# Attention and a mixture of experts on one core: the second LayerNorm's root and scaling on GpSimd, earlier projections, and the first scores among the last expert tiles

## The chip, the cores and the metric

The kernel runs on 1 core of one Trainium2 chip. The metric is the device time of one execution in microseconds; of the kernel before there are three runs, with a median of 300.53 us (299.96 to 301.22). Engines are named as the profile names them: PE (TensorE matmuls), PEld (its weight loads), DVE (VectorE), ACT (ScalarE), POOL (GpSimd), SP (SyncE, which here only issues DMAs). Each engine runs its own list of instructions in order and waits on semaphores.

## The reference, cut to what matters

```
xn  = layernorm(x)                                   # x: 4 batches x 512 tokens x 128
q, k, v = xn @ Wq, xn @ Wk, xn @ Wv
latent  = (k + v) @ W_down_kv                        # 32 wide
k_rec, v_rec = latent @ W_up_k, latent @ W_up_v      # 16 heads of 8
scores  = clip(q k_rec^T * scale) * exp(-1e-4 |i-j|) # per head, 512 x 512
attn    = softmax(scores) @ v_rec;   A = attn @ Wo

logits  = xn @ Wr^T + br;  top 2 of 8 experts, softmax of the two as weights cw
y_e     = gelu(xn @ W1[e]^T + b1[e]) @ W2[e]^T + b2[e]     # 128 -> 512 -> 128
out     = sum_e cw_e * y_e
z       = out + xn
M       = (z - mean(z)) * rsqrt(var(z) + 1e-12) * ln_w + ln_b

result  = x + A + M
```

## The kernel before, in words

**Stages.** First come the first LayerNorm, the transposes, the projections and the routing. Then the experts: the routed tokens are sorted by expert and cut into 39 tiles of 128 rows (`WORK` = 39). Last comes the attention of 4 batches x 16 heads. The second LayerNorm (the `z` of the reference), the output projection and the final sum lie inside the attention stage. A flag computed on the chip says whether scores are small enough for exps without a maximum; it is set here, and the `If` branch runs on each engine. The `Else` branch is a slow general path that isn't run.

**Expert tiles.** For tile i: POOL gathers its rows by an indirect DMA (L307), PE transposes them (`turn_places`, L561), DVE copies them (L964) and copies the expert's weights (`load_panel`, L927), PE multiplies into 512 hidden columns in bank 0 or 1 (`widen`, L572), ACT applies gelu (L774), PE multiplies back into bank 6 or 7 (`narrow`, L583), DVE adds the bias (L972), and SP stores pairs of tiles in DRAM. PE's list is a software pipeline: `widen(n - 1)` stands ahead of `narrow(n - 2)`. After the last bias DVE clears bank 6 (L981), where the attention's outputs will add up.

**The attention loop.** Its unit is one head with two of its four key tiles against all 512 queries; there are 128 units (`UNITS`), and n counts them on every engine. PE computes two products of 128 x 512 into two PSUM banks (`scores`, L626); three pairs of banks are in use (`SCORE_SLOTS`), so `scores(n)` waits until exp n - 3 has read its pair. DVE multiplies parts of both by a correction of the decay (`mend`, L1043). ACT takes the exp of both (L811). PE multiplies with the values, a quad of four units at a time (`outputs`, L645). Every eight units (a group, four heads) ACT copies the sums out (`heads`, L785), PE transposes them (`turn`, L659) and DVE divides (`normalise`, L1031 and L1033), always behind the mend of a unit n with n % 8 = 3. The order is written out by hand: each engine runs through n = 0 to 147 and the lists below say at which n an extra step stands.

**The second LayerNorm, batch by batch.** POOL gathers both expert rows of every token (L316), weighs and adds them and adds xn (`combine_step_of`, L328 to L336; its end is `acc_ready`). DVE takes statistics (`token_stats`, L986, which waits for `acc_ready`) at unit `STATS_AT[b]` and the variance one unit later (`token_variance`, L992 and L994). POOL takes the power -1/2 (`take_root`, L341). DVE refines this root with four instructions on 128 x 4 numbers (`refine_root`, L1000 to L1003) at `SCALE_AT[b]` and scales the four tiles of the batch in two pairs one and two units later (`scale_tokens`, L1007). POOL multiplies by ln_w and adds x + ln_b (`finish_rest`, L346 and L348; its end is `rest_ready`). POOL's list (`close`) also holds the splitting of q and k into bf16 parts for the later batches. It begins with a wait for the last stores of y.

**The output projection.** At `PROJECT_AT[b]` PE transposes the batch's attention (`turn_attention`, L603) and ACT copies it one unit later on its list (L789); at `MULTIPLY_AT[b]`, two units on, PE multiplies by Wo (L610), and one unit later DVE adds it to the rest (`add_projection`, L1014, which waits for `rest_ready`); SP stores the batch. The next `turn` waits for that addition, since both use bank 7.

## Time and profile before

| | before |
|---|---|
| median of 3 runs | 300.53 us |
| the profiled execution's own time | 301.67 us |
| its span, first to last instruction | 299.9 us |
| mean granted TensorE clock | 0.945 |
| busy: PE / PEld | 250.9 us (84%) / 140.1 us (47%) |
| busy: DVE | 227.9 us (76%) |
| busy: ACT | 203.0 us (68%) |
| busy: POOL | 167.9 us (56%) |

The attention loop is everything from about 129 us on. The span is the time that the instructions cover; the execution's own time has a little around it. The busy shares are means over stages that have different limits, so they can't say what one stage waits for; the views below are cut by stage.

### The profile page before, as it was taken

The numbers are of one execution on the slowest core, as the hardware profiler recorded it, in microseconds if no ns is written. First come the engines' busy times: TensorE is split into PE (matmuls) and PEld (weight loads), VectorE is DVE, ScalarE is ACT, GpSimd is POOL, SyncE is SP. The second block draws the span as 40 slices with busy tenths as digits, with TensorE's granted clock in tenths as the row PEclk, the third lists the DMA queues.
The fourth block names the chain that finished last, engine by engine and source line by source line (L and its number), as shares of the span: only waits on it lengthen the run. The fifth ranks groups of instructions, "written<-read, shape, count | busy, mean of one in ns | idle before, by whom it ended". The sixth has DMA issues, their size and how long they took to land.

```text
span 299.9 us, 6073 instructions
## 1 busy us (share of the span) xinstructions
PE 250.9 (84%) x2161; PEld 140.1 (47%) x2185; DVE 227.9 (76%) x585; ACT 203.0 (68%) x348; POOL 167.9 (56%) x158
## 2 busy tenths in 40 slices
PE   0394457989999999969999999989999598969883
PEld 0282033979999999922222233322233023332342
DVE  3718987587777777677888888889889987998831
ACT  1556506446666665668999999988997588769840
POOL 9296707447464557968899999995305711050000
PEclk9998957899999999998999999999999789999996
DMA  6992501242222323125111531115000000000001
GB/s 212 469 388 70 164 21 44 72 159 74 79 70 70 71 71 68 35 88 185 47 35 28 169 96 31 35 52 175 11 2 2 1 0 2 35 7 31 2 35 42
DMA packets 14065, 24.37 MB, mean 81 GB/s; under 512 B 2240, under 2 KB 11104, under 8 KB 13648
## 3 DMA queue, kind: packets, MB, share of 16 engines
q1 hardware_dynamic: 11424, 19.03, 17.8%
q0 software_dynamic: 2272, 4.66, 6.4%
q8 instruction: 19, 0.31, 0.4%
q10 hardware_dynamic: 336, 0.25, 0.3%
q14 instruction: 14, 0.11, 0.1%
HBM read 12.99 MB, written 4.65 MB: 59 GB/s over the span
## 4 chain that ended last, share of the span: by engine, by line
PE 57%; DVE 23%; ACT 11%; issue 5%; DMA 2%; another core or an unknown queue 1%; ACTq 0%; DVEq 0%
PE ps L645 13%; PE ps L626 12%; PE ps L572 11%; PE ps L583 11%; ACT shared L811 9%; DVE ps L1043 8%; PE ps L659 2%; DMA wvl<-w_router 2%; DVE panels L1007 2%; PE ps L493 2%; DVE shared L908 2%; PE ps L561 1%; PE ps L610 1%; PE ps L485 1%; DVE panels L1014 1%
## 5 line engine op out<-in xcount | busy, mean ns | idle before, releaser
L811 ACT ACTIVATE shared<-ps 128x1024 f32<-128x1024 f32 x128 | 124.8, 1029 | 21.3 <-DVE ps L1043 18.6
L1043 DVE TENSOR_TENSOR ps<-ps,mend_sb 128x128 f32<-128x128 f32 (+3 forms) x256 | 112.9, 495 | 19.8 <-PE ps L626 15.3
L626 PE MATMUL ps<-stacked 128*128 128x512 bf16 x232 | 71.5, 392 | 15.1 <-ACT shared L811 12.3
L645 PE MATMUL ps<-shared,v_sb 128*9 128x256 f32 x1024 | 74.5, 388 | 0.0
L774 ACT ACTIVATE shared<-ps,shared 128x128 f32<-128x128 f32 x156 | 44.6, 369 | 32.4 <-PE ps L572 32.4
L307 POOL DMA_INDIRECT shared<-xn_scr,source_i x39 | 42.0, 1076 | 39.1 <-PE ps L561 28.3
L927 DVE COPY shared<-panels 128x1156 f32 x39 | 36.3, 930 | 14.6 <-issue 14.6
L626 PEld LDWEIGHTS ps<-stacked 128*128 128x128 bf16 x256 | 17.1, 98 | 58.8 <-ACT shared L811 36.2
L572 PE MATMUL ps<-shared 128*128 128x128 f32 x312 | 42.3, 279 | 1.3 <-DVE shared L964 1.2
L583 PE MATMUL ps<-shared 128*128 128x128 f32 x312 | 42.2, 279 | 0.3 <-ACT shared L774 0.3
L645 PEld LDWEIGHTS ps<-shared,v_sb 128*9 128x9 f32 x1024 | 18.8, 89 | 48.1 <-issue 36.3
L572 PEld LDWEIGHTS ps<-shared 128*128 128x128 f32 x312 | 38.8, 195 | 2.0 <-DVE shared L964 1.6
L583 PEld LDWEIGHTS ps<-shared 128*128 128x128 f32 x312 | 38.8, 196 | 0.5 <-ACT shared L774 0.5
L316 POOL DMA_INDIRECT panels<-y_scr,y_row x32 | 31.2, 974 | 7.9 <-issue 5.2
L346 POOL TENSOR_TENSOR panels<-panels,rest_sb 128x512 f32<-128x512 f32 x4 | 5.1, 1271 | 31.9 <-DVE panels L1007 31.9
L972 DVE TENSOR_TENSOR y_rows<-ps,shared 128x128 f32<-128x128 f32 x39 | 11.3, 291 | 8.0 <-PE ps L583 7.5
L785 ACT COPY out_heads<-ps 128x512 f32<-128x512 f32 x16 | 9.3, 584 | 6.4 <-PE ps L645 6.4
L659 PE MATMUL ps<-chain_sb,out_heads 128*128 128x128 f32 x64 | 9.7, 275 | 3.1 <-DVE panels L1014 2.3
L561 PE MATMUL ps<-chain_sb,shared 128*128 128x128 f32 x39 | 11.2, 286 | 1.1 <-DMA shared<-xn_scr,source_i 1.1
L749 ACT ACTIVATE qT_sb<-ps 128x512 f32<-128x512 f32 x4 | 2.5, 614 | 14.2 <-PE ps L512 14.2
L964 DVE COPY shared<-ps 128x128 f32<-128x128 f32 x39 | 11.0, 282 | 0.4 <-PE ps L561 0.3
L659 PEld LDWEIGHTS ps<-chain_sb,out_heads 128*128 128x128 f32 x64 | 7.7, 141 | 7.3 <-issue 3.7
(146 smaller groups left out, 245.7 us busy)
## 6 DMA issues: line engine op xcount, KB each, us to landing
stacked<-parts SPq DMA_DIRECT2D x48, 128.0 KB
panels<-weights SPq DMA_DIRECT2D x1, 4624.0 KB, 18.2
y_scr<-y_rows SPq DMA_DIRECT2D x19, 128.0 KB
x_sb<-x_tiles SPq DMA_DIRECT2D x4, 256.0 KB, 4.8
xn_scr<-x_sb SPq DMA_DIRECT2D x1, 1024.0 KB, 7.2
xnT<-x_tiles SPq DMA_DIRECT2D x1, 1024.0 KB
out<-panels SPq DMA_DIRECT2D x4, 256.0 KB, 2.3
shared<-xn_scr,source_i POOLq DMA_INDIRECT x39
```

Source lines behind the costliest of these rows:

```text
L307: nc.gpsimd.indirect_dma_start(x_rows[:, i % X_SLOTS, :], None, xn_scr, bass.IndirectOffsetOnAxis(ap=source_i[:, i:i + 1], axis=0)).then_i ...
L316: nc.gpsimd.indirect_dma_start(gathered[:, c, t, :], None, y_scr, bass.IndirectOffsetOnAxis(ap=y_row[:, at:at + 1], axis=0)).then_inc(y_ba ...
L561: nc.tensor.transpose(ps[:, 4 + i % 2, 0:P], x_rows[:, i % X_SLOTS, :], ident).then_inc(xT_psum, 1)
L572: last = nc.tensor.matmul(ps[:, s, c * P:(c + 1) * P], panel[:, i % 4, c * P:(c + 1) * P], x_cols[:, s, :], start=True, stop=True)
L583: last = nc.tensor.matmul(ps[:, Y_BANKS[i % 2], 0:D], hidden[:, i % 2, c, :], panel[:, i % 4, F + c * D:F + (c + 1) * D], start=(c == 0), ...
L626: nc.tensor.matmul(ps[:, 2 * (n % SCORE_SLOTS) + k, :], k_rows[:, b % 2, h, keys:keys + P], q_rows[:, b % 2, h, :], start=True, stop=True) ...
L645: last = nc.tensor.matmul(ps[32 * g:32 * g + VW, OUT_BANK, queries], v_sb[:, b * QT + tile, h, :], probs_fast[:, quad % 2, g, k * S + quer ...
L659: last = nc.tensor.transpose(ps[:, TURN_BANK, t * P:(t + 1) * P], out_heads[:, t * P:(t + 1) * P], ident)
L774: last = nc.scalar.activation(hidden[:, i % 2, c, :], ps[:, i % 2, c * P:(c + 1) * P], ACT.Gelu, bias=panel[:, i % 4, 2 * F + D + c:2 * F ...
L811: nc.scalar.activation(probs_fast[:, quad % 2, g, :].rearrange("p (k q) -> p k q", k=2), ps[:, 2 * (n % SCORE_SLOTS):2 * (n % SCORE_SLOTS) ...
L927: nc.vector.tensor_copy(panel[:, i % 4:i % 4 + 1, :], panels[:, bass.ds(e, 1), :]).then_inc(panel_ready, 1)
L1043: last = nc.vector.tensor_tensor(scores, scores, mend_sb[:, S - reach:], ALU.mult)
```

## The change: what it does

- The four refining instructions of the root and the four scalings of each batch go from DVE's list to POOL's (`take_root` and `finish_rest`), with waits between them; `SCALE_AT` is gone.
- The statistics stand at units 44, 52, 75 and 82 instead of 58, 66, 92 and 98. The projections of batches 0 to 2 stand at 85, 93 and 109 instead of 101, 109 and 125; that of batch 3 stays at 141. `MULTIPLY_AT` follows by two.
- PE: `scores(0)` stands ahead of `narrow(37)` and `scores(1)` ahead of `narrow(38)`. The pairs of banks are numbered one on, so that units 0 and 1 use banks 2 to 5 and unit 2 banks 0 and 1. DVE: the last two bias additions go behind the read of the flag, with mend 0 and mend 1 behind each; the clearing of bank 6 follows them.
- ACT: a tiny exp stands behind the last gelu, ahead of the wait for the flag.

The diff without the parts of the general path:

```diff
@@ -226,13 +226,16 @@
...
-
-
-        STATS_AT = (58, 66, 92, 98)
-        SCALE_AT = (84, 88, 106, 109)
-        PROJECT_GROUPS = (10, 11, 13)
+        root_step = sem("root_step")
+
+
+        STATS_AT = (44, 52, 75, 82)
+        PROJECT_GROUPS = (8, 9, 11)
         PROJECT_AT = [TURN_AFTER + 2 * GROUP * group + 4 for group in PROJECT_GROUPS] + [UNITS + 3 * GROUP + 1]
         MULTIPLY_AT = [n + 2 for n in PROJECT_AT]
+
+        def score_bank(n):
+            return 2 * ((n + 1) % SCORE_SLOTS)
 
...
 
             def take_root(b):
-                tiles = batch_tiles(b)
+
+                tiles, done = batch_tiles(b), 4 * b
                 pool.wait_ge(z_var, b + 1)
-                nc.gpsimd.tensor_tensor(rstd[:, tiles], newton[:, 0, tiles], minus_half, ALU.pow).then_inc(z_root, 1)
+                nc.gpsimd.tensor_tensor(rstd[:, tiles], newton[:, 0, tiles], minus_half, ALU.pow).then_inc(root_step, 1)
+                pool.wait_ge(root_step, done + 1)
+                nc.gpsimd.tensor_tensor(newton[:, 2, tiles], rstd[:, tiles], rstd[:, tiles], ALU.mult).then_inc(root_step, 1)
+                pool.wait_ge(root_step, done + 2)
+                nc.gpsimd.tensor_tensor(newton[:, 2, tiles], newton[:, 2, tiles], newton[:, 0, tiles], ALU.mult).then_inc(root_step, 1)
+                pool.wait_ge(root_step, done + 3)
+                nc.gpsimd.tensor_scalar(newton[:, 2, tiles], newton[:, 2, tiles], -0.5, 1.5, ALU.mult, ALU.add).then_inc(root_step, 1)
+                pool.wait_ge(root_step, done + 4)
+                nc.gpsimd.tensor_tensor(rstd[:, tiles], rstd[:, tiles], newton[:, 2, tiles], ALU.mult).then_inc(z_root, 1)
 
             def finish_rest(b):
-                tiles = batch_tiles(b)
-                pool.wait_ge(z_scaled, 2 * (b + 1))
-                nc.gpsimd.tensor_tensor(z[:, tiles, :], z[:, tiles, :], wide(ln_w), ALU.mult).then_inc(rest_step, 1)
+                tiles = range(b * QT, (b + 1) * QT)
+                pool.wait_ge(z_root, b + 1)
+                for t in tiles:
+                    nc.gpsimd.tensor_scalar(z[:, t, :], acc[:, t, :], mv[:, t, 0:1], rstd[:, t:t + 1], ALU.subtract, ALU.mult).then_inc(z_scaled, 1)
+                pool.wait_ge(z_scaled, QT * (b + 1))
+                nc.gpsimd.tensor_tensor(z[:, batch_tiles(b), :], z[:, batch_tiles(b), :], wide(ln_w), ALU.mult).then_inc(rest_step, 1)
                 pool.wait_ge(rest_step, b + 1)
-                nc.gpsimd.tensor_tensor(z[:, tiles, :], z[:, tiles, :], x_again[:, tiles, :], ALU.add).then_inc(rest_ready, 1)
+                nc.gpsimd.tensor_tensor(z[:, batch_tiles(b), :], z[:, batch_tiles(b), :], x_again[:, batch_tiles(b), :], ALU.add).then_inc(rest_ready, 1)
 
...
-            for n in range(WORK + 2):
+            for n in range(WORK + 1):
                 if n < WORK:
                     turn_places(n)
-                if 1 <= n < WORK + 1:
+                if n >= 1:
                     widen(n - 1)
-                if n >= 2:
+                if 2 <= n < WORK:
                     narrow(n - 2)
...
@@ -621,9 +636,11 @@
                         pe.wait_ge(rows_in[b % 2], (b // 2 + 1) * len(PRODUCTS) * 2 * 16)
                     if n >= SCORE_SLOTS:
                         pe.wait_ge(fast_probs, n - SCORE_SLOTS + 1)
+                    elif n == 1:
+                        pe.wait_ge(xT_read, WORK)
                     for k in range(2):
                         keys = HALVES[half][k] * P
-                        nc.tensor.matmul(ps[:, 2 * (n % SCORE_SLOTS) + k, :], k_rows[:, b % 2, h, keys:keys + P],
+                        nc.tensor.matmul(ps[:, score_bank(n) + k, :], k_rows[:, b % 2, h, keys:keys + P],
                                          q_rows[:, b % 2, h, :], start=True, stop=True).then_inc(fast_scores, 1)
 
...
 
+
+                scores(0)
+                narrow(WORK - 2)
+                scores(1)
+                narrow(WORK - 1)
                 for n in range(UNITS + 5 * GROUP):
-                    if n < UNITS:
+                    if 2 <= n < UNITS:
                         scores(n)
...
@@ -777,6 +801,8 @@
 
             for i in range(WORK):
                 widened(i)
+
+            nc.scalar.activation(std[0:1, 0:1], std[0:1, 0:1], ACT.Exp)
 
...
                         act.wait_ge(fast_used, quad - 1)
                     nc.scalar.activation(probs_fast[:, quad % 2, g, :].rearrange("p (k q) -> p k q", k=2),
-                                         ps[:, 2 * (n % SCORE_SLOTS):2 * (n % SCORE_SLOTS) + 2, :], ACT.Exp).then_inc(fast_probs, 1)
+                                         ps[:, score_bank(n):score_bank(n) + 2, :], ACT.Exp).then_inc(fast_probs, 1)
...
+            def add_bias(i):
+                v.wait_ge(y_psum, i + 1)
+                if i >= 4 and i % 2 == 0:
+                    v.wait_ge(y_out[i // 2 % 2], 16 * (i // 4))
+                nc.vector.tensor_tensor(y_rows[:, i // 2 % 2, i % 2, :], ps[:, Y_BANKS[i % 2], 0:D], panel[:, i % 4, 2 * F:2 * F + D],
+                                        ALU.add).then_inc(y_read, 1)
+
             norm_maxima(0)
-            for n in range(WORK + 2):
+            for n in range(WORK):
                 if n < WORK:
                     v.wait_ge(xT_psum, n + 1)
                     if n >= 2:
@@ -965,21 +998,13 @@
                 if n + 1 < WORK:
                     load_panel(n + 1)
                 if n >= 2:
-                    i = n - 2
-                    v.wait_ge(y_psum, i + 1)
-                    if i >= 4 and i % 2 == 0:
-                        v.wait_ge(y_out[i // 2 % 2], 16 * (i // 4))
-                    nc.vector.tensor_tensor(y_rows[:, i // 2 % 2, i % 2, :], ps[:, Y_BANKS[i % 2], 0:D], panel[:, i % 4, 2 * F:2 * F + D],
-                                            ALU.add).then_inc(y_read, 1)
+                    add_bias(n - 2)
...
-            v.wait_ge(y_read, WORK)
-            nc.vector.memset(ps[:, OUT_BANK, :], 0.0).then_inc(out_clear, 1)
-
...
-            def refine_root(b):
-                tiles = slice(b * QT, (b + 1) * QT)
-                v.wait_ge(z_root, b + 1)
-                then(nc.vector.tensor_tensor(newton[:, 2, tiles], rstd[:, tiles], rstd[:, tiles], ALU.mult))
-                then(nc.vector.tensor_tensor(newton[:, 2, tiles], newton[:, 2, tiles], newton[:, 0, tiles], ALU.mult))
-                then(nc.vector.tensor_scalar(newton[:, 2, tiles], newton[:, 2, tiles], -0.5, 1.5, ALU.mult, ALU.add))
-                then(nc.vector.tensor_tensor(rstd[:, tiles], rstd[:, tiles], newton[:, 2, tiles], ALU.mult))
-
-            def scale_tokens(b, pair):
-                for t in range(b * QT + 2 * pair, b * QT + 2 * pair + 2):
-                    last = nc.vector.tensor_scalar(z[:, t, :], acc[:, t, :], mv[:, t, 0:1], rstd[:, t:t + 1], ALU.subtract, ALU.mult)
-                last.then_inc(z_scaled, 1)
-
...
             with v.If(fast == 1):
                 v.wait_ge(fold_in, 2 * 16)
+
+                def mend(n):
+                    half = n // GROUP % 2
+                    for k, tile in enumerate(HALVES[half]):
+                        reach = (tile + 1) * P
+                        v.wait_ge(fast_scores, 2 * n + k + 1)
+                        scores = ps[:, score_bank(n) + k, 0:reach]
+                        last = nc.vector.tensor_tensor(scores, scores, mend_sb[:, S - reach:], ALU.mult)
+                    last.then_inc(fast_fixed, 1)
 
...
+                add_bias(WORK - 2)
+                mend(0)
+                add_bias(WORK - 1)
+                mend(1)
+                v.wait_ge(y_read, WORK)
+                nc.vector.memset(ps[:, OUT_BANK, :], 0.0).then_inc(out_clear, 1)
                 for n in range(UNITS + 5 * GROUP):
-                    if n < UNITS:
-                        half = n // GROUP % 2
-                        for k, tile in enumerate(HALVES[half]):
-                            reach = (tile + 1) * P
-                            v.wait_ge(fast_scores, 2 * n + k + 1)
-                            scores = ps[:, 2 * (n % SCORE_SLOTS) + k, 0:reach]
-                            last = nc.vector.tensor_tensor(scores, scores, mend_sb[:, S - reach:], ALU.mult)
-                        last.then_inc(fast_fixed, 1)
+                    if 2 <= n < UNITS:
+                        mend(n)
                     group, at = divmod(n - TURN_AFTER, 2 * GROUP)
                     if 0 <= group < GROUPS and at == 2:
                         normalise(group)
@@ -1049,14 +1065,11 @@
                         token_stats(b)
                     if (b := batch_at(n, STATS_AT, 1)) is not None:
                         token_variance(b)
-                    if (b := batch_at(n, SCALE_AT)) is not None:
-                        refine_root(b)
-                    for pair in range(2):
-                        if (b := batch_at(n, SCALE_AT, pair + 1)) is not None:
-                            scale_tokens(b, pair)
                     if (b := batch_at(n, MULTIPLY_AT, 1)) is not None:
                         add_projection(b)
...
```

## Rows read from the trace of the kernel before

**Rows 1.** The page's chain of work that ended last: shares of the span by engine.
```profile
PE 57%; DVE 23%; ACT 11%; issue 5%; DMA 2%; another core or an unknown queue 1%; ACTq 0%; DVEq 0%
```

**Rows 2.** Busy time by stretch; columns: stretch, length, busy (count) per engine, PEclk, DMA, GB/s.
```profile
core 0: us, PE busy (x) PEld busy (x) DVE busy (x) ACT busy (x) POOL busy (x), PEclk, DMA share, GB/s
157.18:166.05 8.87, 8.53 (x84) 2.69 (x85) 7.55 (x18) 8.25 (x9) 8.20 (x9) 1.00 0.14 39
192.83:202.10 9.27, 8.46 (x84) 2.56 (x84) 8.51 (x27) 8.16 (x9) 8.71 (x10) 1.00 0.16 42
202.10:211.50 9.40, 8.50 (x84) 2.64 (x85) 8.51 (x27) 8.23 (x9) 6.21 (x7) 1.00 0.47 155
211.50:277.80 66.30, 56.99 (x520) 18.88 (x529) 59.19 (x160) 51.32 (x56) 17.76 (x15) 0.95 0.03 9
244.65:256.84 12.19, 10.97 (x102) 4.66 (x102) 9.95 (x30) 9.75 (x11) 1.01 (x1) 1.00 0.01 1
```

**Rows 3.** Timeline 123 to 135 us: start, busy, engine, line, operation, count, [idle before].
```profile
127.59 1.16 PE L583 MATMUL ps<-shared 128*128 128x128 f32 x8 [0.34 <-ACT shared L774]
128.79 0.29 DVE L972 TENSOR_TENSOR y_rows<-ps,shared 128x128 f32<-128x128 f32 x1 [1.21 <-PE ps L583]
129.26 0.48 DVE L981 MEMSET ps<- 128x512 f32 x1 [0.18 <-DVE y_rows L972]
130.29 4.29 DVE L1043 TENSOR_TENSOR ps<-ps,mend_sb 128x128 f32<-128x128 f32 x10 [0.54 <-PE ps L626]
```

**Rows 4.** The page's group of the score products: busy, mean ns of one.
```profile
L626 PE MATMUL ps<-stacked 128*128 128x512 bf16 x232 | 71.5, 392 | 15.1 <-ACT shared L811 12.3
```

**Rows 5.** Timeline of ACT in the attention loop.
```profile
131.22 6.52 ACT L811 ACTIVATE shared<-ps 128x1024 f32<-128x1024 f32 x7 [2.38 <-DVE ps L1043]
...
283.15 0.59 ACT L789 COPY kT_sb<-ps 128x512 f32<-128x512 f32 x1 [0.36 <-PE ps L603]
```

**Rows 6.** DVE's groups from 129 us on: busy us, mean ns of one, idle before.
```profile
L1007 DVE TENSOR_SCALAR panels<-x_sb,mv,rstd 128x128 f32<-128x128 f32 x16 | 5.9, 409 | 0.0
...
L1002 DVE TENSOR_SCALAR newton<-newton 128x4 f32<-128x4 f32 x4 | 2.4, 612 | 0.1
L1000 DVE TENSOR_TENSOR newton<-rstd 128x4 f32<-128x4 f32 x4 | 2.2, 543 | 0.0
...
L1001 DVE TENSOR_TENSOR newton<-newton 128x4 f32<-128x4 f32 x4 | 1.4, 362 | 0.1
...
L1003 DVE TENSOR_TENSOR rstd<-rstd,newton 128x4 f32<-128x4 f32 x4 | 0.6, 162 | 0.1
```

**Rows 7.** Timeline of PE behind the last exps.
```profile
286.24 1.16 PE L610 MATMUL ps<-rest_sb,kT_sb 128*128 128x128 f32 x8
...
288.83 1.91 PE L645 MATMUL ps<-shared,v_sb 128*9 128x256 f32 x32
```

**Rows 8.** Timeline of DVE in the attention loop.
```profile
197.12 0.17 DVE L994 TENSOR_SCALAR newton<-mv 128x4 f32<-128x4 f32 x1
...
214.71 0.29 DVE L1033 TENSOR_TENSOR qT_sb<-ps,inv_fast 128x128 f32<-128x128 f32 x1
...
220.51 1.78 DVE L1043 TENSOR_TENSOR ps<-ps,mend_sb 128x128 f32<-128x128 f32 x4 [0.17 <-PE ps L626]
...
229.79 1.22 DVE L1000 TENSOR_TENSOR newton<-rstd 128x4 f32<-128x4 f32 x1
```

**Rows 9.** Timeline of POOL in the attention loop.
```profile
206.78 1.02 POOL L341 TENSOR_TENSOR rstd<-newton,top 128x4 f32<-128x4 f32 x1 [2.96 <-DVE newton L994]
207.77 2.04 POOL L328 TENSOR_TENSOR panels<-panels,top 128x512 f32<-128x512 f32 x2
...
211.25 1.27 POOL L336 TENSOR_TENSOR x_sb<-x_sb,panels 128x512 f32<-128x512 f32 x1
```

**Rows 10.** POOL's groups over the span, three of them.
```profile
L346 POOL TENSOR_TENSOR panels<-panels,rest_sb 128x512 f32<-128x512 f32 x4 | 5.1, 1271 | 31.9 <-DVE panels L1007 31.9
...
L262 POOL CAST counting_b<-rest_sb 128x128 bf16<-128x128 f32 x1 | 0.3, 297 | 0.0
...
L258 POOL MEMSET top<- 128x4 f32 x1 | 0.2, 160 | 0.0
```

More of the change, by code:

```diff
@@ L677, in _ @@
             with pe.Else():
+                narrow(WORK - 2)
+                narrow(WORK - 1)
                 pe.wait_ge(y_read, WORK)
@@ L1015, in add_projection @@
                                         ALU.add).then_inc(out_ready, 1)
-            def rescale(b):
-                refine_root(b)
-                for pair in range(2):
-                    scale_tokens(b, pair)
             fast = v.value_load(flag[0:1, 0:1], min_val=0, max_val=1)
@@ L1051, in _ @@
                         token_variance(b)
-                    if (b := batch_at(n, SCALE_AT)) is not None:
-                        refine_root(b)
-                    for pair in range(2):
-                        if (b := batch_at(n, SCALE_AT, pair + 1)) is not None:
-                            scale_tokens(b, pair)
                     if (b := batch_at(n, MULTIPLY_AT, 1)) is not None:
@@ L1059, in _ @@
             with v.Else():
+                add_bias(WORK - 2)
+                add_bias(WORK - 1)
                 v.wait_ge(decay_in, 16)
@@ L1085, in _ @@
                     token_variance(b)
-                    if b:
-                        rescale(b - 1)
-                rescale(B - 1)
                 for b in range(B):
```

## The prediction

> **What bounds the kernel now.** I read the chain of waits first, by engine: PE has over half of it, DVE 23%, ACT 11% [rows 1]. The first 129 us (routing, then 39 expert tiles on PE) are not made shorter here; the change acts on the attention loop behind them, so I cut that into stretches from one first exp of a group of eight units to the next [rows 2]. A quiet group (157.18 to 166.05) takes 8.87 us: ACT is busy 8.25 us, PE 8.53 us, DVE 7.55 us. There ACT and PE bound it together and DVE has about 1 us to spare. Where one batch's statistics are added (192.83 and 202.10), the group takes 9.27 and 9.40 us, 0.40 and 0.53 us more. From unit 72 to unit 120 the loop takes 66.30 us where six quiet groups would take 6 x 8.87 = 53.2 us. Of its 66.30 us DVE is busy 59.19 us. So DVE's extra work, in order between the mends that every exp waits for, is what makes this stretch 13.1 us too long. The profiled execution took 301.67 us, 1.8 us more than its span of 299.9 us and 1.1 us more than the median of the runs, 300.53 us; I make the sum against the first and carry the difference to the median.
>
> **Start of the loop.** Before, narrow(38) ends at 127.59 + 1.16 = 128.75, DVE adds the last bias (128.79, 0.29 us), clears the output bank (129.26, 0.48 us), stands 0.54 us, and mends unit 0 from 130.29 [rows 3]; PE's first score products were long issued, so I read the 0.54 us as DVE's read of the flag and its branch. The first exp starts at 131.22, then they follow 0.93 us apart (7 in 6.52 us with the last at 1.02) [rows 5]. Now scores(0) and scores(1) each go ahead of a narrow, two products of 0.39 us each that overlap partly [rows 4]: estimate 0.6 us a pair. PE's idle 0.34 us ahead of narrow(38) takes part of it: the last narrow ends at 128.75 + 1.2 - 0.34 = 129.6. DVE reads the flag while it waits for narrow(37), so the 0.54 us goes. Its order becomes bias 37, mend 0 (two instructions, about 0.85 us), bias 38 until 129.95, mend 1 until 130.8, clearing until 131.25, mend 2 until 132.1, mend 3 until 132.95. Exp 3 starts there; before it started at 131.22 + 3 x 0.93 = 134.0. Gain 1.0 us (bounds: 0 if the extra products ahead of the narrows cost their full time and clearing, 2.1 if all exps follow the first as early as it can come: narrow(37) ends by 129.6 - 1.16 - 0.6 = 127.85, its bias and mend 0 at about 129.1, against 131.22). The load of ACT's exp table is done before ACT's wait of 2.38 us for mend 0 begins [rows 5], and the explicit tiny exp leaves it there: cost nothing; what is left of that wait hides it, and without it the tiny exp would cost about what a small copy does, 0.2 us (the 128x4 additions of DVE take 0.17 us). The last bias add is 0.9 us later; behind it wait the last store of y and POOL's first gather, so POOL's whole chain starts 0.9 us later.
>
> **Root and scaling leave DVE.** It removes 4 instructions of 0.54, 0.36, 0.61 and 0.16 us mean for each of four batches, and 16 scalings that add up to 5.9 us [rows 6]: 2.2 + 1.4 + 2.4 + 0.6 + 5.9 = 12.5 us of DVE. They stand in groups that DVE bounds (what it can't absorb there is the path). What remains between units 72 and 120 is statistics of two batches and now three projections. One projection costs, besides the add on DVE, 8 matmul passes in PE's order (1.16 us [rows 7]) and a copy on ACT (0.59 us). I price it from the stretch from exp 96 to exp 105, which holds one projection and one statistics: 12.19 us [rows 2] against 8.87 + 1.02 = 9.89 us, so 2.30 us, less 0.45 us for statistics: 1.85 us (bounds 0.95 us, the copy alone as below, and 2.4 us). Statistics of batch 2 now stand directly behind a normalise (unit 75), those of batch 3 right before one; I take 0.6 us for each (bounds 0.4 and 1.4, all of their DVE time). Six groups: 53.2 + 1.2 + 3 x 1.85 = 59.95 us.
>
> **Whether DVE's new waits fill.** token_stats(2) moves from unit 92 to 75 and token_stats(3) from 98 to 82; behind each wait stand all mends, so a late POOL stops DVE, ACT and PE. Before, DVE is through the normalise of unit 75 at 214.71 + 0.29 = 215.0, and through mend 82 at 220.51 + 1.78 = 222.3 [rows 8]. Now 1.0 us earlier by the start: 214.0, and 222.3 - 1.0 + 0.6 = 221.9. POOL: acc(2) was ready at 211.25 + 1.27 = 212.52 [rows 9]. Its wait of 2.96 us for the second variance falls away, since that comes 13 units earlier; the late start adds 0.9 us; two batches of four refining instructions of 128x4 are new. No such POOL instruction is in the trace. Below is the 128x4 memset, 0.16 us; above, the power on 128x4, 1.02 us [rows 9, 10]. I take 0.2 us, near the memset, and 0.06 us between, 2.1 us for eight. acc(2): 212.5 - 3.0 + 0.9 + 2.1 = 212.6, 1.4 us in time. Then finish_rest(0): four scalings of 128x128, between a 128x128 cast of 0.30 us and a full 128x512 multiply of 1.27 us [rows 10]; I take 0.35 us, as one operand only is streamed. 4 x 0.41 + 2 x 1.33 = 4.3 us. The combining of batch 3 takes as long as that of batch 2, 207.77 to 212.52 [rows 9], 4.75 us. acc(3): 212.6 + 4.3 + 4.8 = 221.7, against 221.9. So this wait is just filled; I charge 0.2 us. The waits of units 44 and 52 stand later against their accumulations than these two and cost nothing by the same timelines; rest_ready(0) follows at 212.6 + 4.3 = 216.9, before DVE is at unit 82, and its add stands at unit 88: nothing, unless POOL is over 10 us late. The SP queue only sees its output stores earlier.
>
> **What goes from the end.** The copy of batch 2 leaves group 15, where it delayed the exps by the 0.36 us that ACT stood for PE's transposes and its own 0.59 us, 0.95 us [rows 5]: gain 0.9. Its multiply stood at 286.24, ahead of the last score-value products, and the add held the turn behind it [rows 7]. Those 32 products started at 288.83; they need only the last exp. The exps behind the copy start 0.11 us before its end, at 283.63, and four in a row take 3 x 0.93 + 1.02 = 3.8 us, so it ends at 287.4. Gain 288.83 - 287.45 = 1.4, of which I count 1.3. The last projection stays where it is.
>
> Sum: 1.0 + (66.3 - 59.95 - 0.2 = 6.1) + 0.9 + 1.3 = 9.3 us. 301.67 - 9.3 = 292.4 for a profiled execution, 300.53 - 9.3 = 291.2 for the median.
>
> **A rule that speaks against it.** DVE's refinements, all of 4 columns, were uneven: the first has a mean of 0.54 us, the last 0.16 us [rows 6], and the one at 229.79 took 1.22 us, while the small add for the variance took 0.17 us at 197.12 [rows 8]. The Trainium skill, page "SBUF — State Buffer", section "Who interferes with whom", says that a DVE instruction with two SBUF inputs, or one like a single-input tensor_scalar that can use both ports, is held until POOL's running instruction is done. By that rule the four variance adds, which now all fall into POOL's busy time, are each held for up to one POOL instruction. That is priced as a rival.
>
> **Rivals.** (a) *POOL's small instructions are dearer, moderately*: at 0.5 us for each of the twelve that lie ahead of acc(3) the excess is 8 x 0.3 + 4 x 0.15 = 3.0 us, nearly all waited for by DVE at units 75 and 82: 294.2. The power's 1.02 us speaks for it, the casts against. Chance 0.14. (b) *The slower side, the same place*: POOL has a floor per arithmetic instruction whatever its width. At 1.27 us, a full multiply [rows 10], the twelve cost 15.2 us instead of 3.0, DVE stands 12.2 us, and the kernel takes 303.4. It decides from about 1.03 us each, (9.3 + 3.0) / 12. For it: the power on four columns. Against: 0.30 us for the 128x128 cast. Chance 0.05. (c) *Variance adds held by POOL*: four times half to all of 1.1 us: 2 to 4 us less gain, 294.3. For: the uneven refinements. Against: 0.17 us before. Chance 0.08. (d) *PE becomes the bound*: with 8.53 of 8.87 us busy, three projections in five groups cost 2.4 us each and the earlier start is lost behind the narrows: 2.7 us less gain, 293.9. Chance 0.10. (e) *The start change does nothing it says*: only the root and the projections count, 292.2; inside the forecast's own range.
>
> **How the numbers follow.** The forecast, 289 to 293, has 0.63. The range reaches to (a), (c) and (d) and to a cheaper projection on the low side (three at 1.0 us, 288.7): 288.5 to 296.0. What measurement can tell from no change is 0.5%, 1.5 us. Faster than that: the forecast and (a), (c), (d), less a tail, 0.92; within it, a POOL instruction at about 0.9 to 1.15 us, 0.04; slower, 0.04.
>
> **What would show it.** Right: first exp near 129.2 but exp 3 near 133; no refining or scaling on DVE; groups from unit 40 to 72 as now; DVE's longest wait before its statistics of batches 2 and 3 under 1 us; units 72 to 120 in about 60 us; the last 32 products about 9 us earlier. Wrong: POOL's four-column multiply above 0.5 us, a wait of several us at unit 75 or 82, or a granted clock below 1 for PE in that stretch.

## The result and the profile after

The changed kernel takes 293.13 us (median of 4, 292.92 to 293.47) against 300.88 us before (4 runs): a ratio of 0.9747 with a 95% interval of 0.9719 to 0.9775. That is 7.75 us faster; I had forecast 9.3 us and 291.2 us, with a range from 288.5 to 296.0. On another chip the same kernel had a ratio of 0.9742 (0.9715 to 0.9768).

The profiled execution has a span of 291.0 us, 8.9 us shorter. One of these belongs to no edit: the last gelu began at 126.39 before and at 125.39 after, ahead of everything that was changed. Over all the traces below it began between 125.00 and 127.21 us, so two spans can differ by 2 us before the changed code is reached. The stretches, cut as in [rows 2] from one first exp of a group to the next:

```profile
core 0: us, PE busy (x) PEld busy (x) DVE busy (x) ACT busy (x) POOL busy (x), PEclk, DMA share, GB/s
153.72:162.59 8.87, 8.75 (x86) 2.70 (x85) 7.54 (x18) 8.25 (x9) 8.11 (x8) 1.00 0.19 48
...
171.47:207.18 35.71, 35.20 (x338) 10.66 (x337) 32.27 (x90) 32.78 (x36) 32.82 (x40) 1.00 0.25 74
207.18:271.07 63.89, 57.70 (x542) 20.14 (x541) 49.28 (x129) 51.42 (x57) 34.10 (x41) 1.00 0.04 13
250.83:261.62 10.79, 10.17 (x98) 4.07 (x96) 7.65 (x19) 8.83 (x10) 0.00 (x0) 1.00 0.01 2
261.62:271.07 9.45, 8.95 (x86) 2.67 (x85) 8.04 (x19) 8.36 (x9) 0.00 (x0) 1.00 0.07 28
271.07:279.74 8.67, 8.47 (x86) 2.93 (x84) 6.68 (x17) 8.24 (x9) 0.00 (x0) 1.00 0.01 2
```

The quiet group is unchanged at 8.87 us. Units 72 to 120 (the line 207.18:271.07) take 63.89 us, where they took 66.30; I had forecast 60.2 us. Units 40 to 72 (171.47:207.18) take 35.71 us; before they took 36.6 us (174.93 to 211.50), and the forecast counted no gain there. DVE's work in units 72 to 120 fell from 59.19 to 49.28 us, and yet the stretch is 10.7 us longer than six quiet groups. The two lines 250.83:261.62 and 261.62:271.07 hold one projection and nothing else: 20.24 us for two groups, 2.50 us above quiet. Three of them make 7.5 us. The remaining 3.2 us are the statistics, and nearly all of it is this, in the timeline of POOL, DVE and ACT of the changed kernel:

```profile
210.74 3.14 POOL L359 TENSOR_SCALAR panels<-x_sb,mv,rstd 128x128 f32<-128x128 f32 x4
213.96 1.28 POOL L361 TENSOR_TENSOR panels<-panels,rest_sb 128x512 f32<-128x512 f32 x1
...
220.01 1.27 POOL L339 TENSOR_TENSOR x_sb<-x_sb,panels 128x512 f32<-128x512 f32 x1
...
221.32 0.87 DVE L1011 BATCH_NORM_STATS2 stats<-x_sb 128x6 f32<-128x128 f32 x4 [2.81 <-POOL x_sb L339]
...
223.16 1.02 ACT L837 ACTIVATE shared<-ps 128x1024 f32<-128x1024 f32 x1 [3.54 <-DVE ps L1040]
```

POOL scales batch 0 (L359) before it combines batch 3 (its end is L339). DVE stands 2.81 us at unit 82 for that sum, and ACT 3.54 us behind DVE. What POOL's new instructions cost, of its groups:

```profile
L359 POOL TENSOR_SCALAR panels<-x_sb,mv,rstd 128x128 f32<-128x128 f32 x16 | 12.5, 792 | 0.0
...
L347 POOL TENSOR_TENSOR newton<-rstd 128x4 f32<-128x4 f32 x4 | 0.8, 200 | 0.3
```

The refining instructions take 0.20 us, as estimated; a scaling takes 0.79 us, not 0.35.

The start in ACT's timeline, first of the kernel before (the last gelus, and exp 8, which begins at 139.88), then of the changed one:

```profile
126.39 1.14 ACT L774 ACTIVATE shared<-ps,shared 128x128 f32<-128x128 f32 x4 [0.64 <-PE ps L572]
...
139.88 3.03 ACT L811 ACTIVATE shared<-ps 128x1024 f32<-128x1024 f32 x3 [0.52 <-PE ps L645]
```

```profile
125.39 1.14 ACT L798 ACTIVATE shared<-ps,shared 128x128 f32<-128x128 f32 x4 [0.65 <-PE ps L587]
...
127.95 1.00 ACT L837 ACTIVATE shared<-ps 128x1024 f32<-128x1024 f32 x1
129.16 1.02 ACT L837 ACTIVATE shared<-ps 128x1024 f32<-128x1024 f32 x1 [0.22 <-DVE ps L1040]
130.44 5.61 ACT L837 ACTIVATE shared<-ps 128x1024 f32<-128x1024 f32 x6 [0.26 <-DVE ps L1040]
136.42 3.94 ACT L837 ACTIVATE shared<-ps 128x1024 f32<-128x1024 f32 x4 [0.37 <-DVE ps L1040]
```

From the last gelu to exp 8 this is 136.42 - 125.39 = 11.0 us, where it was 139.88 - 126.39 = 13.5 us: 2.5 us gained in this one execution. The experiments show that this is not what the start is worth in general.

### The profile page after: what moved, and what is told of

It reads as the page before. It is cut to its first block, busy times and chain, and to the rows that moved or that the text cites. A ratio compares the mean times of both kernels' runs of the same rounds, so it can differ in the third digit from the quotient of the medians.

```text
span 291.0 us, 6096 instructions
## 1 busy us (share of the span) xinstructions
PE 249.3 (86%) x2185; PEld 140.1 (48%) x2185; DVE 216.9 (75%) x553; ACT 202.5 (70%) x349; POOL 183.0 (63%) x190
## 4 chain that ended last, share of the span: by engine, by line
PE 66%; DVE 14%; ACT 10%; issue 5%; DMA 3%; POOL 0%; ACTq 0%; DVEq 0%
PE ps L662 17%; PE ps L643 15%; PE ps L587 12%; PE ps L598 11%; ACT shared L837 8%; PE ps L676 2%; DVE ps L1040 2%; PE ps L625 2%; DMA wvl<-w_router 2%; PE ps L508 2%; PE ps L576 2%; DVE shared L934 2%; PE ps L500 1%; DVE panels L1026 1%; DMA shared<-xn_scr,source_i 1%
## 5 line engine op out<-in xcount | busy, mean ns | idle before, releaser
L643 PE MATMUL ps<-stacked 128*128 128x512 bf16 x256 | 75.0, 383 | 6.1 <-ACT shared L837 4.8
L662 PE MATMUL ps<-shared,v_sb 128*9 128x256 f32 x1024 | 72.7, 381 | 0.1
L319 POOL DMA_INDIRECT panels<-y_scr,y_row x32 | 30.9, 965 | 8.2 <-issue 4.8
L359 POOL TENSOR_SCALAR panels<-x_sb,mv,rstd 128x128 f32<-128x128 f32 x16 | 12.5, 792 | 0.0
L296 POOL TENSOR_TENSOR parts<-folded,parts 128x512 bf16<-128x512 f32 x8 | 10.4, 1303 | 0.5
```

Of the source, the lines that this page charges most:

```text
L319: nc.gpsimd.indirect_dma_start(gathered[:, c, t, :], None, y_scr, bass.IndirectOffsetOnAxis(ap=y_row[:, at:at + 1], axis=0)).then_inc(y_ba ...
L643: nc.tensor.matmul(ps[:, score_bank(n) + k, :], k_rows[:, b % 2, h, keys:keys + P], q_rows[:, b % 2, h, :], start=True, stop=True).then_in ...
L662: last = nc.tensor.matmul(ps[32 * g:32 * g + VW, OUT_BANK, queries], v_sb[:, b * QT + tile, h, :], probs_fast[:, quad % 2, g, k * S + quer ...
```

## Experiments

Every kernel was timed beside the kernel before; ratios are to that, smaller is faster. The control and e1 to e3 ran on one chip, e4 to e7 on a second, e8 to e11 on a third. There is one trace of each kernel, so what a trace shows holds for that execution.

| kernel | median us | before us | ratio (95% interval) |
|---|---|---|---|
| control, the change again | 293.84 | 301.45 | 0.9742 (0.9715 to 0.9768) |
| e1 new order on POOL | 292.92 | 301.45 | 0.9709 (0.9681 to 0.9737) |
| e2 statistics of batch 3 at unit 90 | 293.19 | 301.45 | 0.9727 (0.9700 to 0.9754) |
| e3 the start part alone | 301.95 | 301.45 | 1.0019 (0.9999 to 1.0039) |
| e4 start alone, adds on POOL | 297.87 | 301.24 | 0.9909 (0.9881 to 0.9936) |
| e5 order, adds on POOL | 290.50 | 301.24 | 0.9640 (0.9611 to 0.9669) |
| e6 order, projection in halves | 291.16 | 301.24 | 0.9687 (0.9661 to 0.9713) |
| e7 the change without its start | 293.22 | 301.24 | 0.9742 (0.9720 to 0.9763) |
| e8 adds on POOL alone | 293.97 | 301.49 | 0.9729 (0.9675 to 0.9782) |
| e9 as e5 without the start part | 291.84 | 301.49 | 0.9680 (0.9621 to 0.9739) |
| e10 as e5, batch 2's projection late | 291.31 | 301.49 | 0.9649 (0.9595 to 0.9703) |
| e11 as e5, DVE copies attention | 289.73 | 301.49 | 0.9589 (0.9537 to 0.9642) |

### The control

> The changed kernel once more, as the yardstick for its siblings on the same chip. Both theories: 7.0 to 8.5 us faster than before; DVE waits about 2.8 us for batch 3's sum at unit 82, and the last first-group exps start about 2.4 us sooner after the last gelu than before.

7.6 us faster, as expected. The two other things that I expected didn't come: exp 8 began only 0.8 us sooner after the last gelu than before (12.7 against 13.5 us), and the profile doesn't show the 2.8 us wait at unit 82. DVE came there later instead, for two reasons. One is the start. The other is that of its four variance adds (L1019), which read and write 128 x 4 numbers, two were long.

```profile
180.75 0.65 DVE L1019 TENSOR_SCALAR newton<-mv 128x4 f32<-128x4 f32 x1
190.60 0.17 DVE L1019 TENSOR_SCALAR newton<-mv 128x4 f32<-128x4 f32 x1
216.28 1.13 DVE L1019 TENSOR_SCALAR newton<-mv 128x4 f32<-128x4 f32 x1
225.12 0.17 DVE L1019 TENSOR_SCALAR newton<-mv 128x4 f32<-128x4 f32 x1
```

Counted from the last gelu, POOL's sum of batch 3 came at 95.8 us in this trace (222.09) and at 95.9 us in the first (221.28), but DVE was ready for it at 96.3 us (222.53) instead of 93.1 us (218.51). Of these 3.2 us the start made 1.7 us (12.7 against 11.0 us to exp 8), and units 40 to 56, with the first long add, 1.0 us (19.34 against 18.38 us). So what I had seen in one trace was one of several ways in which the kernel can lose the same time.

### e1 and e2: take the wait at unit 82 away

```diff
                 for at in range(4):
                     combine_step_of(2, at)
-                finish_rest(0)
                 for at in range(4):
                     combine_step_of(3, at)
+                finish_rest(0)
                 finish_rest(1)
```

> POOL combines batch 3 before it scales batch 0; nothing else changes. Theory A (POOL's scalings, 0.79 us each instead of the 0.35 us I took, make batch 3's sum late, and the 2.8 us that DVE then waits at unit 82 is lost for good): the sum is ready 5.8 us sooner, the wait is gone, 2.3 to 2.9 us faster than the changed kernel. Rival B (PE, busy 8.75 of 8.87 us in a quiet group, is the bound there and the wait only swallows slack): under 0.5 us faster.

```diff
-        STATS_AT = (44, 52, 75, 82)
+        STATS_AT = (44, 52, 75, 90)
```

> Statistics of batch 3 at unit 90 instead of 82; POOL's list is as in the change. Theory A: the wait is gone as well, 2.0 to 2.9 us faster than the changed kernel, a little less than with the new order if the statistics cost more among the projections. Rival B: under 0.5 us faster. If this gains and the new order doesn't, POOL's order has a cost of its own.

Neither theory's number came. In both traces DVE never waits for POOL's sum, and yet e1 is only 0.9 us faster than the control in the medians and e2 0.7 us; the intervals overlap. In e2's trace the adds of batches 0 and 2 took 1.16 us each. In the traces of the control and of e7 (below), which have POOL's old order too, DVE comes behind the sum and doesn't wait, so there the 2.8 us were not there to be had. How many executions are like these and how many like the first, no run shows.

Even the 0.9 us of e1 can't be put down to the order. In its trace, against the control's, units 72 to 120 are 0.7 us shorter (61.08 against 61.80 us), but 0.9 us come behind the last exp (10.18 against 11.04 us), mostly in the last multiply by Wo. It ran at a mean granted clock of 0.56 in the control (first two lines) and of 1.00 in e1 (last line):

```profile
286.58 1.88 PE L625 MATMUL ps<-rest_sb,kT_sb 128*128 128x128 f32 x8 [0.68 <-ACT kT_sb L815]
286.58:288.46 1.88, 1.87 (x8) 1.58 (x8) 0.00 (x0) 0.00 (x0) 0.00 (x0) 0.56 0.05 13
```

```profile
286.35 1.16 PE L625 MATMUL ps<-rest_sb,kT_sb 128*128 128x128 f32 x8 [0.68 <-ACT kT_sb L815]
```

These eight passes took 1.88 to 2.08 us in six of the fourteen traces (before, after, the control, e2, e3, e8) and 1.16 us in the others. What decides it isn't shown; it is 0.7 to 0.9 us that no edit here aimed at.

### e3 and e4: the start part alone

> The kernel before with only the change at the loop's start (first products among the narrows, flag read early, tiny exp). My prediction's term: 1.0 us faster than before. Theory C (the start also keeps PE's clock up and spares its first half-clock products, as the changed trace has it: 2.4 us from the last gelu to exp 8): 2.0 to 2.6 us faster than before. Rival: the start's gain is given back at the first group boundary, under 0.5 us.

It gained nothing: 1.0019. Its trace is of the slowest of its twelve runs (303.86 us, 1.9 us above their median), and shows where that one lost its gain; whether the others lost it in the same way isn't shown. One variance add (here L1007), behind the normalise of unit 59:

```profile
196.58 1.38 DVE L1007 TENSOR_SCALAR newton<-mv 128x4 f32<-128x4 f32 x1
196.65 1.28 POOL L284 TENSOR_TENSOR folded<-kT_sb,fold_sb 128x512 f32<-128x512 f32 x1
...
197.88 3.32 DVE L1055 TENSOR_TENSOR ps<-ps,mend_sb 128x256 f32<-128x256 f32 x8
...
198.80 2.86 ACT L825 ACTIVATE shared<-ps 128x1024 f32<-128x1024 f32 x3 [1.48 <-DVE ps L1055]
...
199.88 0.61 PE L631 MATMUL ps<-stacked 128*128 128x512 bf16 x2 [1.80 <-ACT shared L825]
200.41 1.00 PE L650 MATMUL ps<-shared,v_sb 128*9 128x256 f32 x8
```

The add ends at 197.96, 0.03 us after POOL's multiply at 197.93; before the change the same add took 0.17 us, since DVE came to it while POOL was issuing an indirect DMA (197.05 to 198.04; the add is in [rows 8]). This is the lock of the Trainium skill, page "SBUF — State Buffer", section "Who interferes with whom": of a DVE instruction in a two-port mode and a GpSimd instruction, the one that is issued second is blocked until the other ends. The trace agrees with it at the end, to 0.03 us; by the records the add began 0.07 us ahead of the multiply. Of the 32 variance adds on DVE in all traces eleven took over 0.18 us (0.23 to 1.38 us), and each of them ended 0.02 to 0.04 us behind an arithmetic instruction of POOL. One doesn't fit: at 223.92 in the changed kernel an add took 0.17 us while POOL's scaling ran from 223.59 to 224.39. In e3 ACT then stands 1.48 us, PE 1.80 us, and PE's clock falls; in stretches of the same trace:

```profile
183.28:192.16 8.88, 8.76 (x86) 2.70 (x85) 7.54 (x18) 8.26 (x10) 8.17 (x9) 1.00 0.12 33
192.16:204.27 12.11, 10.31 (x85) 2.73 (x84) 9.80 (x27) 8.24 (x9) 11.29 (x13) 0.86 0.21 60
200.40:203.20 2.80, 2.80 (x23) 0.64 (x26) 1.10 (x3) 2.17 (x3) 2.78 (x4) 0.52 0.36 104
```

The granted clock is 0.52 in the mean from 200.40 to 203.20, nearly all of it at the level of 1.2 GHz, and eight products with the values take 1.00 us instead of 0.62. The group takes 12.11 us where it took 9.27 us before [rows 2]: one held add of four columns goes with 2.8 us. e4 takes the adds off DVE:

```diff
-                then(last)
-                nc.vector.tensor_scalar(newton[:, 0, ...], mv[:, ..., 1], 1e-12, None, ALU.add).then_inc(z_var, 1)
+                last.then_inc(z_var, 1)
...
                 pool.wait_ge(z_var, b + 1)
+                nc.gpsimd.tensor_scalar(newton[:, 0, tiles], mv[:, tiles, 1], 1e-12, None, ALU.add).then_inc(root_step, 1)
+                pool.wait_ge(root_step, ...)
```

> The kernel before with the start part, as in the run before, and with the four variance adds (128x4, + 1e-12) moved from DVE to POOL. Theory D: the start part alone gained nothing since one variance add of DVE, 0.17 us before, took 1.38 us, until POOL's multiply was through; ACT and PE stood behind it, PE's clock fell, and 2.9 us were lost between units 56 and 72. Without an add on DVE the stretch 56 to 72 takes 18 to 19 us again and the kernel is 1.0 to 2.5 us faster than before. Rival E (the start's gain is never one; it is jitter of the first group): still within 0.7 us of before.

0.9909: 2.7 us faster than before by the ratio and 3.4 us in the medians, at the upper end of theory D or a little above; rival E falls. Units 56 to 72 took 18.37 us in its trace, as theory D has it, against 21.59 us in e3's. The adds and the start part are not separated here (there is no run of the kernel before with the adds alone on POOL), but e3 and e4 differ by the adds only, and by 1.1%, on two chips.

### e7 and e9: the start part taken out

> The change without its start part. My prediction's terms: 1.0 us slower than the whole change. If the start part is worth its 2.4 us of the first changed trace: 2.4 us slower. If it is worth nothing on the chip, as alone: within 0.6 us of the whole change.

```diff
-                scores(0)
-                narrow(WORK - 2)
-                scores(1)
-                narrow(WORK - 1)
...
-                add_bias(WORK - 2)
-                mend(0)
-                add_bias(WORK - 1)
-                mend(1)
```

0.9742, the same as the whole change; by the intervals, on two chips, a difference of up to about 1 us could hide in it. The traces show how a gain at the start can end at nothing: counted from the last gelu, unit 40 began 0.65 us sooner in the control than in e7 (47.84 against 48.49 us), and unit 56 began 0.4 us later (67.18 against 66.78 us), and between the two stands the variance add that was held in the control (0.65 us) and free in e7 (0.17 us). On a kernel whose POOL waits and holds are cured the start part may be worth something:

> New order and adds on POOL, but the loop's start as before the change. If the start part earns its place only once nothing behind it stands in wait for POOL: 1.0 to 2.5 us slower than with the start part. If it is worth nothing anywhere: within 0.6 us.

0.9680 against 0.9640 for e5, 1.2 us in the ratios, within both intervals, and on another chip: not settled by the times. The two traces speak for 1.0 us, what I had forecast: counted from the last gelu, e5 is 0.96 us ahead of e9 at unit 40 (47.60 against 48.56 us) and still 0.95 us at unit 120 (144.16 against 145.11 us).

The traces show why the 2.5 us of the first one is not the rule. From the last gelu to exp 8 the changed start took 11.0 us in three traces (the first one, e4, e6) and 11.6 to 12.8 us in the eight others; the old start took 13.3 to 13.5 us (before, e7, e9). The slow ones differ among themselves. In e1 (12.8 us) the granted clock was 0.84 in the mean between 129 and 140 us. In the control (12.7 us) it was 1.00 there, as in the first trace, but ahead of 138.97 ACT stood 2.06 us and ahead of 140.05 PE stood 1.47 us, and the profile names no engine for either wait. What brings them about stays open.

### e5, e8: order and adds together

> The new order on POOL (combine batch 3 first) and the variance adds on POOL. Theory D: the held adds of the change's own executions (up to 1.1 us each) are gone: 0.8 to 2.0 us faster than the run with the new order alone. Rival: POOL gets 0.27 us longer four times and nothing else changes, within 0.4 us of it.

0.9640: 2.1 us faster than the order alone, and 3.1 us faster than the change by the ratios; the intervals of e5 and of the control and e1 don't touch. Theory D's upper end is met, but between chips. On e5's own chip the kernel with the order and without the adds is e6, whose projections are split as well: it is only 0.7 us slower in the medians and 1.4 us by the ratios, with intervals that overlap. And e7, the change without its start, is 2.7 us slower than e5 there. In the traces e5 is shorter than the control by 1.3 us in units 40 to 56 (18.00 against 19.34 us), by 0.7 us in units 72 to 120 (61.07 against 61.80 us), both stretches with a held add in the control, and by 0.9 us behind the last exp, the clock's part again.

> The change with only the variance adds moved to POOL, POOL's order as in the change. Theory D (a held add costs up to 1.1 us and more behind it): 1.0 to 2.0 us faster than the change. But theory A adds: DVE is then earlier at unit 82 and stands there for batch 3's sum, so less than the 2.1 us that the adds gave on top of the new order: 0.5 to 1.5 us. If it gives the full 2.1 us, POOL's lateness never mattered.

The adds alone give nothing that shows (0.9729 against 0.9742), less than the 0.5 us at the lower end of what I gave for A and D together; the interval, 0.9675 to 0.9782, is wide enough for 1.5 us. The trace of e8, in which nothing is held any more, has the wait back, all of it:

```profile
221.72 1.27 POOL L339 TENSOR_TENSOR x_sb<-x_sb,panels 128x512 f32<-128x512 f32 x1
...
223.03 0.87 DVE L1013 BATCH_NORM_STATS2 stats<-x_sb 128x6 f32<-128x128 f32 x4 [2.82 <-POOL x_sb L339]
```

The adds also made POOL itself later: counted from the last gelu the sum came at 97.0 us (223.00), 1.1 us behind that of the control. So several causes lie one behind the other: what DVE has lost ahead of unit 82, to held adds or at the start, it does not wait there, and what it wins ahead of it it waits. Each cure alone gives under 1.1 us, both together 3.1 us between chips. On one chip, e10 (both cures; its batch 2 projection is late) is 2.7 us faster than e8, and its slowest run, 292.36 us, lies below e8's fastest, 292.63 us.

### e6, e10, e11: what a projection costs

```diff
+                        project_attention(b, range(QT if b == B - 1 else QT // 2))
+                    if (b := batch_at(n, MULTIPLY_AT, 1)) is not None and b < B - 1:
+                        project_attention(b, range(QT // 2, QT))
```

> The new order, and the multiply by Wo of the first three projections in two halves, the second one unit later. Theory F (a projection costs 2.5 us, since its 8 passes stand ahead of one unit's scores and DVE waits 1.6 us for them): halves of 0.55 us each hide partly, 0.3 to 1.0 us less per projection, 1 to 3 us in all against the new order alone. Rival G (PE is full, the passes cost the same wherever they stand): within 0.5 us.

0.9687 against 0.9709 for e1: inside the intervals, on two chips. In the trace units 104 to 120 took 20.39 us against 20.25 us, and units 88 to 104, with another split projection, 21.56 us against 20.82 us in e1 and in every other trace that has this projection unsplit with ACT's copy. The split gives nothing that shows, and theory F's 1 to 3 us did not come; that PE is full, rival G's reason, isn't shown by it.

```diff
-        PROJECT_GROUPS = (8, 9, 11)
+        PROJECT_GROUPS = (8, 9, 13)
```

> New order and adds on POOL, with batch 2's projection back at unit 125. My prediction: the move forward is worth 0.9 + 1.3 = 2.2 us at the end and costs 1.85 us in the loop, so this is 0.3 us slower. By the changed trace it costs 2.5 us in the loop: 0.3 us faster. Both within what can be told; more than 1 us either way says that the cost or the gain of the move was read wrong.

0.9649 against 0.9640: the same, as far as can be told (e10's interval alone is 1.6 us to either side), and as both sums said. Its trace gives the terms. Without a projection units 104 to 120 took 272.82 - 255.08 = 17.74 us from one copy of the heads to the second next, twice a quiet group to the hundredth, so a projection costs 20.24 - 17.74 = 2.50 us; the move earns back about 2.3 us at the end.

```profile
255.08 0.58 ACT L813 COPY out_heads<-ps 128x512 f32<-128x512 f32 x1 [0.34 <-PE ps L664]
...
263.95 0.58 ACT L813 COPY out_heads<-ps 128x512 f32<-128x512 f32 x1 [0.34 <-PE ps L664]
...
272.82 0.59 ACT L813 COPY out_heads<-ps 128x512 f32<-128x512 f32 x1 [0.34 <-PE ps L664]
```

```diff
-                    if (b := batch_at(n, PROJECT_AT, -1)) is not None:
-                        copy_attention(b)
...
+                    if (b := batch_at(n, PROJECT_AT, 1)) is not None:
+                        v.wait_ge(attnT_psum, b + 1)
+                        nc.vector.tensor_copy(attnT[:, b * QT:(b + 1) * QT, :], ...).then_inc(attnT_ready, 1)
```

> New order and adds on POOL, and DVE instead of ACT copies the transposed attention (four copies). Theory H (ACT bounds the loop, DVE has 1.3 us a group to spare since the root and the scaling left it): 0.3 to 0.95 us less for each of three projections, 1 to 3 us faster than without. Rival: the copy stands ahead of a mend that an exp waits for, 0.6 us each go back: within 0.6 us.

289.73 us, ratio 0.9589 (0.9537 to 0.9642), the fastest of all and 11.8 us faster than before. All its runs (288.40 to 289.93) lie below all runs of e10 on the same chip (289.97 to 292.36), which differs also in the place of batch 2's projection. Against e5, on another chip, it is 1.5 us by the ratios, and the intervals overlap. The traces show the gain plainly: units 72 to 120 take 59.06 us against 61.07 us in e5. In its trace the exps of a projection's group:

```profile
254.44 4.03 ACT L837 ACTIVATE shared<-ps 128x1024 f32<-128x1024 f32 x4
259.66 1.02 ACT L837 ACTIVATE shared<-ps 128x1024 f32<-128x1024 f32 x1 [1.19 <-DVE ps L1038]
...
269.11 4.07 ACT L837 ACTIVATE shared<-ps 128x1024 f32<-128x1024 f32 x4 [0.20 <-DVE ps L1038]
```

ACT goes from its copy of the heads straight on. Units 104 to 120 (249.56 to 269.11) take 19.55 us, so a projection costs 1.81 us instead of 2.50; the 1.19 us that ACT stands behind PE's eight passes are still there.

## Why the prediction came out as it did

The sign and the range held: the medians differ by 7.75 us where I had 9.3 us, and 293.13 us lies just outside the band of 289 to 293. That the total came so near is in part luck. In the first trace the largest term, units 72 to 120, gave 2.4 us instead of 6.1 us. What made up for most of it stood in no term of mine: 1.0 us ahead of all edits, 1.5 us more at the start than I had, and 0.9 us in units 40 to 72. With the two terms at the end as forecast that makes the 8.9 us of this trace.

- **Whether DVE's new waits fill: the step that was furthest off.** "As one operand only is streamed" I took 0.35 us for a scaling on POOL and charged 0.2 us for the wait at unit 82. A scaling measured 0.79 us; four of them are 1.8 us later, and DVE stood 2.81 us. The scalings are not all of it. Counted from the last gelu, POOL's sum came only 0.6 us later than I had it (its list was 0.9 us ahead of my sum at batch 2), and DVE was ready 2.4 us sooner, by the two gains that I had not counted. My rival (a) was the first half of this mechanism. The bounds of 0.30 and 1.27 us held it, and I chose the wrong neighbour: the cast has one arithmetic step and no per-row operands, the scaling two steps with two.
- **Variance adds held by POOL, rival (c), chance 0.08.** It happened: 0.65 and 1.13 us in the control, 0.62 in e1, 1.16 twice in e2, 1.38 in e3, 1.21 in e6, 1.11 in e7. I priced it at the hold itself; in e3 what stands behind it (ACT, then PE, then the clock) made 2.8 us of one hold. I called (a) and (c) rivals; they share one slack, so they neither add up nor exclude each other.
- **A projection: 1.85 us, measured 2.50.** The stretch I priced it from ended at exp 105. The group behind a projection is still 0.58 us long (9.45 against 8.87 us): the cost ended after my window did. Three of them are 2.0 us. That is close to the price I had given to rival (d), 2.4 us.
- **Statistics: 0.6 us each, measured about 0.2.** Units 72 to 88 had 3.17 us more than quiet besides the projection, of which 2.81 is the wait.
- The wait, the projections and the statistics make up the loop's stretch: 59.95 + 1.95 + 2.81 - 0.84 = 63.87 us, measured 63.89. No variance add was held for long in this trace.
- **What I read past in the kernel before.** I put all 13.1 us that units 72 to 120 took beyond quiet groups down to DVE's extra work. The row that I read them from has a mean clock of 0.95 [rows 2]. PE had stood 2.38 us, until 235.25, behind DVE's refinements and scalings, and then this line of the same trace shows the level of 1.2 GHz:

```profile
235.90:242.70 6.80, 5.27 (x29) 0.81 (x27) 6.70 (x25) 5.00 (x6) 3.56 (x3) 0.50 0.00 1
```

  The three traces with the refinements on DVE (before, e3, e4) have such a stretch of 6.8 us between units 72 and 120, the eleven with them on POOL have none there. So part of what the change gives is the clock; how much, no run separates.
- **The start: 1.0 us.** First exp and exp 3 came a little sooner than worked out (2.6 and 6.0 us after the last gelu, where 2.7 and 6.6 were worked out). From exp 3 to exp 8 another 0.9 us went in the first trace (5.1 instead of 5.9 us); there the granted clock was 1.00 in the mean between 129 and 140 us, where it was 0.84 before. Timed, the part shows nothing in this kernel (e7) and nothing alone (e3); with the other cures the traces have the forecast 1.0 us (e5, e9). My sum took an earlier start as a shift of the whole loop; but DVE's list is tied to POOL's in time, and the shift moved its adds under POOL's multiplies and its statistics ahead of POOL's sums.
- **The end.** The copy of batch 2: group 15 has 8.67 us of exps to the end instead of 287.41 - 277.80 = 9.61, 0.94 us, as forecast 0.9. The tail from the last exp to the last copy of attention: 4.70 us against 6.06, 1.36 us, as forecast 1.3.

## What to carry to other kernels

When two engines' lists are tied by waits in both directions, a gain on one is only a gain up to the next thing it waits for: ask after each edit which wait is now filled, and be ready for two cures to show only together. Price a moved instruction by one with the same number of steps and operands, and price an extra stage by a window that runs on until the pace is the quiet one again. Don't leave even a four-column instruction that shares a port with another engine on the engine that everything waits for; and compare two traces of the same kernel before believing a difference of 1 or 2 us between two kernels, counting from an event ahead of the change and with the granted clock of each stretch beside it.

## What the runs showed of the hardware

- POOL's tensor_scalar with subtract and multiply by per-row numbers takes 0.79 us for 128x128, while a multiply of four times as many columns takes 1.05 to 1.28 us and an instruction of 128x4 0.20 us. The power on 128x4 takes 1.02 us: it is the power that is dear, not the instruction.
- A DVE tensor_scalar of 128x4 from SBUF to SBUF took 0.17 us free and up to 1.38 us beside POOL's arithmetic, ending with POOL's instruction (the exception stands under e3). Beside POOL's indirect DMAs (L319) it took 0.17 us, six times of six. The statistics (L1011, 0.27 to 0.30 us each) and the mends, which have one operand in PSUM (0.40 to 0.51 us for 128x256), were never held like this.
- PE's granted clock is no plain function of one stand. In e3 PE stood 1.80 us at 199.88 and the clock was 0.52 from 200.40 to 203.20; in the changed kernel PE stood up to 2.19 us behind DVE's wait at unit 82, and the clock stayed at 1.00 from 221 to 228. In the kernel before PE stood 2.38 us, until 235.25, and the clock was 0.50 from 235.90 to 242.70. What sets these apart the runs don't show.
